# Eight experts of a GNN and FFN kernel: the low halves of the weights all on VectorE, and SiLU in one ScalarE instruction

## What is computed

```python
x1 = x @ W1 + b1                                   # W1: 1024 x 512 for each of 8 experts
x2 = jnp.clip(x @ W2 + b2, -20.0, 20.0)            # W2: 1024 x 512
hidden = jnp.clip(x1 * (x2 * jax.nn.sigmoid(x2)), -10000.0, 10000.0)
return jnp.clip(hidden @ Wo + bo, -10000.0, 10000.0)   # Wo: 512 x 1024
```

## Time and profile before

| what | value |
|---|---|
| median of 3 runs | 579.73 us (577.4 to 579.78) |
| span of the profiled execution | 574.8 us |
| TensorE busy | 514.5 us (89%) |
| VectorE busy | 430.0 us (75%) |
| ScalarE busy | 280.2 us (49%) |
| GpSimd busy | 234.6 us (41%) |

### The profile page before, as it was taken

The page is one execution under the profiler, slowest core; times in us unless marked ns, Lnnn a source line. Parts: engine busy times, 40 slices in busy tenths (PEclk is TensorE's granted clock), DMA queues, the critical chain, the costliest instruction groups (busy, mean ns, idle before and its releaser), DMA issues.

```text
span 574.8 us, 6831 instructions
## 1 busy us (share of the span) xinstructions
PE 514.5 (89%) x2579; PEld 444.6 (77%) x2579; DVE 430.0 (75%) x669; ACT 280.2 (49%) x406; POOL 234.6 (41%) x143
## 2 busy tenths in 40 slices
PE   3899999999999998989988886579999999996994
PEld 3899889999999997878877674456777676674773
DVE  6558977734433345889997776866999999997996
ACT  3425313332332235767775013329669659647630
POOL 5000433333333411122226712323686696690762
PEclk9999999999999999889999979569999999998889
DMA  8289763343344331020016233574888988984632
GB/s 315 94 282 343 234 260 121 121 146 98 125 147 146 128 137 70 1 74 1 1 58 210 114 111 109 196 285 175 328 322 310 388 313 324 391 298 180 220 110 111
DMA packets 20929, 106.32 MB, mean 185 GB/s; under 512 B 4720, under 2 KB 5104, under 8 KB 11168
## 3 DMA queue, kind: packets, MB, share of 16 engines
q1 hardware_dynamic: 15328, 91.53, 42.7%
q0 software_dynamic: 3696, 7.96, 4.2%
q10 hardware_dynamic: 1872, 6.39, 3.6%
HBM read 98.96 MB, written 6.91 MB: 184 GB/s over the span
## 4 chain that ended last, share of the span: by engine, by line
PE 52%; DVE 28%; issue 8%; ACT 5%; POOL 4%; DMA 1%; DVEq 0%; ACTq 0%; POOLq 0%
PE ps L1115 46%; DVE lo L728 11%; DVE sg L1031 4%; PE ps L1178 3%; POOL xres L480 2%; PE ps L1218 1%; ACT hi L561 1%; DVE xres L1047 1%; ACT xg L645 1%; DVE y L1001 1%; DVE hh L1038 1%; DVE x2c L1027 1%; DVE xg_lo L988 1%; DVE ht_lo L993 1%; ACT sg L654 1%
## 5 line engine op out<-in xcount | busy, mean ns | idle before, releaser
L728 DVE TENSOR_TENSOR lo<-raw,hi 128x2048 fp32r<-128x2048 f32 x58 | 153.8, 2668 | 54.8 <-ACT hi L561 54.6
L561 ACT ACTIVATE hi<-raw 128x2048 fp32r<-128x2048 f32 x70 | 131.8, 1913 | 77.0 <-PE ps L1115 65.0
L447 POOL DMA_INDIRECT mask_rows<-colf,bits x48 | 55.9, 1164 | 134.7 <-DMA mask_rows<-colf,bits 82.1
L489 POOL TENSOR_TENSOR lo<-raw,hi 128x2048 fp32r<-128x2048 f32 x12 | 64.9, 5408 | 50.5 <-ACT hi L561 50.4
L1115 PE MATMUL ps<-xt_hi,hi 128*128 128x384 f32 x192 | 65.2, 340 | 2.2 <-DVE xt_lo L744 2.2
L1115 PE MATMUL ps<-xt_lo,hi 128*128 128x384 f32 x192 | 65.1, 339 | 0.0
L1115 PE MATMUL ps<-xt_hi,lo 128*128 128x384 f32 x192 | 64.9, 338 | 0.0
L1115 PE MATMUL ps<-hi,xg_hi 128*128 128x512 f32 x128 | 54.3, 425 | 7.2 <-DVE lo L728 5.7
L1115 PE MATMUL ps<-lo,xg_hi 128*128 128x512 f32 x128 | 52.3, 409 | 0.0
L1115 PE MATMUL ps<-hi,xg_lo 128*128 128x512 f32 x128 | 52.2, 408 | 0.0
L455 POOL TENSOR_SCALAR pr<-pr,small 128x384 f32<-128x384 f32 x16 | 19.9, 1246 | 75.0 <-DVE small L853 75.0
(11 more groups left out here) (209 smaller groups left out, 1131.1 us busy)
## 6 DMA issues: line engine op xcount, KB each, us to landing
raw<-in_wf SPq DMA_DIRECT2D x42, 1024.0 KB, 6.3
raw<-in_wg SPq DMA_DIRECT2D x28, 1024.0 KB, 5.5
xfb<-in_wf SPq DMA_DIRECT2D x6, 1024.0 KB, 5.8
src_i<-in_srcb ACTq DMA_DIRECT2D x4, 768.0 KB, 6.2
dst_i<-in_dstb ACTq DMA_DIRECT2D x4, 768.0 KB, 9.0
y_rows<-y SPq DMA_DIRECT2D x6, 512.0 KB, 2.9
xin<-in_x SPq DMA_DIRECT2D x3, 512.0 KB, 4.4
xres<-in_x SPq DMA_DIRECT2D x3, 512.0 KB, 4.2
```

Of the source, the lines that this page charges most:

```text
L447: pool.indirect_dma_start(out=mbuf[:, :], out_offset=bass.IndirectOffsetOnAxis(ap=bits[:, 1, g:g + 1], axis=0), in_=colf[:, 5, g:g + 1], i ...
L489: pool.tensor_tensor(lo[SLOT[c]][:, :], raws[RAW[c]], f32(hi[SLOT[c]][:, :]), ALU.subtract).then_inc(pool_lo_done, 1)
L561: act.activation(hi[SLOT[c]][:, :], raws[RAW[c]], ACT.Copy).then_inc(hi_done, 1)
L728: dve.tensor_tensor(lo[SLOT[c]][:, :], raws[RAW[c]], f32(hi[SLOT[c]][:, :]), ALU.subtract).then_inc(lo_done, 1)
```

## The change

The set `POOL_LO` goes away: all six chunks of a turn are made on VectorE, and GpSimd keeps its gathers, its selections and the two additions at the end. `Sigmoid` on ScalarE becomes `Silu`, and VectorE's product of `x2c` and the sigmoid goes away. In VectorE's loop n2 stands behind the clip as the code already had it, and n3 is moved from behind `hh` to a place ahead of it, behind `xg_lo`. A branch for experts with over 128 tokens is changed in the same way.

```diff
-LO_ON_POOL = (1, 4)
-POOL_LO = {c for c in range(FIRST, CHUNKS - 3) if (c - FIRST) % 6 in LO_ON_POOL} | {CHUNKS - 2}
         def wait_lo(engine, c):
-            engine.wait_ge(pool_lo_done if c in POOL_LO else lo_done, nth(c))
+            engine.wait_ge(lo_done, c + 1)
...
-            def split_lo(c):
-                pool.wait_ge(hi_done, c + 1)
-                pool.tensor_tensor(lo[SLOT[c]][:, :], raws[RAW[c]], f32(hi[SLOT[c]][:, :]), ALU.subtract).then_inc(pool_lo_done, 1)
...
-                for c in range(f0(e) + 3, min(f0(e) + 9, CHUNKS)):
-                    if c in POOL_LO:
-                        split_lo(c)
...
-            def sigmoid(e):
+            def silu(e):
                 act.wait_ge(x2_clipped, e + 1)
-                act.activation(sg[:, :], x2c[:, :], ACT.Sigmoid).then_inc(sig_done, 1)
+                act.activation(sg[:, :], x2c[:, :], ACT.Silu).then_inc(silu_done, 1)
...
-                nxt = [k if FIRST <= k < CHUNKS and k not in POOL_LO else None for k in range(f0(e) + 3, f0(e) + 9)]
+                nxt = [k if FIRST <= k < CHUNKS else None for k in range(f0(e) + 3, f0(e) + 9)]
...
                 if nxt[2]:
                     split_lo(nxt[2])
-                dve.wait_ge(sig_done, e + 1)
-                link(dve.tensor_tensor(sg[:, :], x2c[:, :], sg[:, :], ALU.mult))
                 if e + 1 < NE:
                     tokens_lo(e + 1, (e + 1) % 2)
+                if nxt[3]:
+                    split_lo(nxt[3])
+                dve.wait_ge(silu_done, e + 1)
                 dve.wait_ge(chunk_used, up_chunks(e) + 4)
                 if e:
                     dve.wait_ge(h_turned, e)
                 link(dve.tensor_tensor(hh[:, :], B[0], sg[:, :], ALU.mult))
                 dve.tensor_scalar(hh[:, :], hh[:, :], 10000.0, -10000.0, ALU.min, ALU.max).then_inc(h_ready, 1)
-                for k in nxt[3:6]:
+                for k in nxt[4:6]:
                     if k:
                         split_lo(k)
```

More of the change, by code:

```diff
@@ L90 @@
 LAST = (NE - 2, NE - 1)
-POOL_LO = {c for c in range(FIRST, CHUNKS - 3) if (c - FIRST) % 6 in LO_ON_POOL} | {CHUNKS - 2}
-def nth(c):
-    return sum(1 for k in range(c + 1) if (k in POOL_LO) == (c in POOL_LO))
 def before(c):
@@ L232, in gnn_ffn @@
         hi_done, lo_done, chunk_used = sem("hi_done"), sem("lo_done"), sem("chunk_used")
-        pool_lo_done = sem("pool_lo_done")
         x_in = [sem(f"x_in{t}") for t in range(NT)]
@@ L256, in gnn_ffn @@
         xg_turned, xg_scaled, xg_hi_done, xg_lo_done = sem("xg_turned"), sem("xg_scaled"), sem("xg_hi_done"), sem("xg_lo_done")
-        x2_clipped, sig_done, h_ready, h_turned, ht_hi_done, ht_lo_done = (
-            sem("x2_clipped"), sem("sig_done"), sem("h_ready"), sem("h_turned"), sem("ht_hi_done"), sem("ht_lo_done"))
+        x2_clipped, silu_done, h_ready, h_turned, ht_hi_done, ht_lo_done = (
+            sem("x2_clipped"), sem("silu_done"), sem("h_ready"), sem("h_turned"), sem("ht_hi_done"), sem("ht_lo_done"))
         y_ready, y_stored = sem("y_ready"), [sem("y_stored0"), sem("y_stored1")]
@@ L267, in gnn_ffn @@
         over_sel, over_turned, over_hi, over_lo = sem("over_sel"), sem("over_turned"), sem("over_hi"), sem("over_lo")
-        over_up, over_clipped, over_sig, over_h = sem("over_up"), sem("over_clipped"), sem("over_sig"), sem("over_h")
+        over_up, over_clipped, over_silu, over_h = sem("over_up"), sem("over_clipped"), sem("over_silu"), sem("over_h")
         over_scaled, over_h_turned, over_h_hi, over_h_lo, over_down, over_added = (
@@ L668, in _ @@
                         split_hi(k)
-                sigmoid(e)
+                silu(e)
                 if e + 1 < NE:
@@ L711, in _ @@
                     act.wait_ge(over_clipped, step)
-                    act.activation(sg[:, :], x2c[:, :], ACT.Sigmoid).then_inc(over_sig, 1)
+                    act.activation(sg[:, :], x2c[:, :], ACT.Silu).then_inc(over_silu, 1)
                     act.wait_ge(over_h_turned, step)
@@ L1091, in _ @@
                     dve.tensor_scalar(x2c[:, :], B[1], 20.0, -20.0, ALU.min, ALU.max).then_inc(over_clipped, 1)
-                    dve.wait_ge(over_sig, step)
-                    dve.tensor_tensor(sg[:, :], x2c[:, :], sg[:, :], ALU.mult).then_inc(over_dve, 1)
-                    dve.wait_ge(over_dve, e * (3 * (NT - 1)) + (3 * t - 2))
+                    dve.wait_ge(over_silu, step)
                     dve.tensor_tensor(hh[:, :], B[0], sg[:, :], ALU.mult).then_inc(over_dve, 1)
-                    dve.wait_ge(over_dve, e * (3 * (NT - 1)) + (3 * t - 1))
+                    dve.wait_ge(over_dve, e * (2 * (NT - 1)) + (2 * t - 1))
                     dve.tensor_scalar(hh[:, :], hh[:, :], 10000.0, -10000.0, ALU.min, ALU.max).then_inc(over_h, 1)
@@ L1103, in _ @@
                                       ALU.min, ALU.max).then_inc(over_dve, 1)
-                    dve.wait_ge(over_dve, e * (3 * (NT - 1)) + 3 * t)
+                    dve.wait_ge(over_dve, e * (2 * (NT - 1)) + 2 * t)
                     dve.scalar_tensor_tensor(out=xres[:, t, :], in0=y[:, 0, :], scalar=fr[:, t, 7:8],
```

## The result

The changed kernel takes 569.44 us in the median (567.67 to 570.18, 4 runs), the one before 578.70 in the same series (577.40 to 579.78, 4 runs). The ratio is 0.984 with a 95% interval of 0.9819 to 0.9861: 9.3 us, 1.6%, faster. The forecast was 572.7 with a range of 566.5 to 576.5, so the sign and the range held and the size was 7.0 for 9.3 us.

What follows compares the result with a forecast made beforehand. The prediction took a ring through VectorE and ScalarE to bound each turn, at 21.1 us for 21.8. ht_lo 9.5 us earlier, less 2.5 given back at the end, made 7.0: 579.73 to 572.7 us, range 566.5 to 576.5.

Steps and rivals of the forecast that it cites:

- The reading of the long rows: In the expert turns, VectorE's long low halves and product wait for GpSimd's instructions: 2.8 and 4.05 us a turn.
- The rival on the other side: Long VectorE rows belong to its own instructions: 22 us slower, 602; chance 0.07 together with late transfers.
- The ring: Each expert turn: a loop through VectorE and ScalarE, with n3's high half before hh, sets 21.1 us for 21.8.
- SiLU and the table load: On ScalarE: SiLU costs 0.63 us like the sigmoid; the added 1.28 us table load hides in a wait, costing nothing.
- The positions: Where turns lie: x2c of turn 7 at 533.3, 8.1 us earlier; ht_lo at 542.2 to 542.3, 9.5 earlier.
- The step that failed: From ht_lo to the last clips: 10.4 less 2.15 plus 4.6 for collisions with GpSimd's additions, 12.9 us.
- over long before: At the end: TensorE's last block starts behind y at about 543.6 and finishes long before VectorE's last clips.
- Rival 1: At the end: no collision or cheap ones, ScalarE's scaling perhaps late; up to 4.6 us better, 568.1; chance 0.15.
- The distance to the median: Whole kernel: the median of the runs lies 4.9 us above the profiled execution's span, and that distance is kept.

Runs made afterwards that it cites:

- e1: Kernel before with only SiLU in place of sigmoid and product, low halves left on GpSimd and n3 behind hh: 574.85 us, ratio 0.9933.
- e4: Changed kernel with the low halves n2, n5 and that of turn 7 back on GpSimd, SiLU and order kept: 582.51 us, ratio 1.0052.
- e5: Changed kernel with the low half n2 alone back on GpSimd: 587.14 us, ratio 1.0158.
- e2: Kernel before with the halves moved to VectorE and n3 ahead of hh, sigmoid and product kept: 568.35 us, ratio 0.9829.
- e6: Changed kernel with the low half n5 alone back on GpSimd: 577.15 us, ratio 0.9973.
- e3: Changed kernel with n3 put back behind hh: 562.96 us, ratio 0.9731; run once more, 564.41 us, ratio 0.9754.
- e7: Changed kernel with ten more unused 128x128 transposes on TensorE ahead of its last block: 568.64 us, ratio 0.9845.

## Why the prediction was right, and where it was not

**The reading of the long rows** was right. The product of 4.74 us and the pair of 7.30 were waits for GpSimd: both are gone with GpSimd's halves, and e1 and e4 show the wait on whichever instruction of VectorE stands in its way, nearly always one with two inputs in SBUF. The rival on the other side, that the long rows belonged to their own instructions, gave 602 and is refuted by the result. The lock that the Trainium skill describes (SBUF — State Buffer, "SBUF: two separate sides"), exclusive and held for the whole instruction, agrees with the meetings shown here: e5's n1 waited 4.4 us, nearly a full GpSimd half.

**The ring** was right to 0.1 us: 21.1 forecast, 21.11 to 21.18 measured, and its parts are confirmed by e2 (0.69 us of VectorE added inside the waiting, no effect), e6 (2.2 us removed and a meeting of 2.8 put in, 21.72) and e3 (n3's high half taken out: 20.15, with TensorE busy throughout). TensorE waits where the prediction said, at the transposes of `hh`, but for 0.9 us and not 0.6: the 20.5 that it was said to need, its busy time in a turn of before, is 20.15 in e3. What I did not say is that the ring is a cost of the change: the order with n3 behind `hh` is open to the same kernel and 5 to 6 us faster.

**SiLU and the table load** were right at 0.63 us and nothing.

**The positions** held. x2c of turn 7 lies at 535.41, less the 1.8 us of the attention layer 533.6, for the forecast 533.3. ht_lo lies at 544.22, less 1.8 542.4, for 542.2 to 542.3. The regular turns give little of the gain, 1.5 us from turn 1 to turn 5. The rest is the step from turn 0 to turn 1 (1.6), that from turn 5 to turn 6 with its pair (5.2), and the stretch from x2c of turn 6 to ht_lo (1.0), where TensorE decides in both kernels.

**The step that failed** is the end: 12.9 us from ht_lo to the last clips, of which 4.6 for two full meetings of the row additions. It measured 10.1 (554.33 less 544.22), with none in it that cost VectorE time. I took the gathered rows to lie there when ScalarE came to them; they landed 3.20 us later than that. By the rows two things made them late: the gathers themselves waited for VectorE's two-input instructions, up to 2.0 us each (2.96 for 0.94), which the forecast had left out, and the rows landed 2.5 us behind the last of them. ScalarE's scaling began at 550.6, and GpSimd's additions at 551.82, within VectorE's last row addition (551.18 to 552.46), for whose end GpSimd seems to have waited: its two took 5.37 for some 4.6. The meeting that VectorE felt then fell behind the clips, at 1.2 us, not 4.6. In its place came something that the prediction had called "over long before": TensorE's last block, 7.4 us with part of it at half clock, for which VectorE waited 1.88 us. The rows of before have the same block ending 10.0 us behind ht_lo (561.8 less 551.80), and 0.4 us ahead of the clips; it lies hidden only as long as VectorE loses time in meetings. e7 takes most of that wait away and shows a meeting of 2.1 us behind it.

From ht_lo to the end of the span it is 23.3 us for 23.0 before, so the end gave back 0.3 us where 2.5 had been put; that is the 7.0 for 9.1. Rival 1, fewer meetings at the end (568.1), had the reason right, ScalarE's late scaling, but it is as far off in size, 11.6 us for 9.3. That the forecast came out nearly as well as it did is in part luck: the meetings it counted on were not there, and a wait of 1.88 us that it had ruled out took some of their place.

**The distance to the median** was misread too. I took 4.9 us as what lies around the span. It is 1.7, and the rest is that the profiled execution was a short one, with a higher clock in the attention layer. It did not enter the forecast of the difference.

## What to carry to other kernels

A simple instruction that takes many times as long as its neighbours of the same size is waiting inside itself: look at what GpSimd does in that moment, and do not count its length as work of its engine, nor as what deleting it would gain. Moving work off GpSimd pays by the meetings it removes, also where the receiving engine looks nearly full. When several things are changed at once, run each alone: here one line, an empty `POOL_LO`, was 15 us faster than before, and the three parts together 9. When work is put into an engine's queue, walk the ring that each instruction closes through the other engines: here the place of one low half, ahead of or behind `hh`, was worth 5 to 6 us, for the 9.3 of the whole change.

## What the runs showed of the hardware that was not expected

- A meeting depends on the phase. The same 128x2048 half on GpSimd cost a turn 0 or 4.4 us (e5: 21.1 and 25.5), by whether it began 0.2 us before or behind the point at which VectorE changed instructions. At the end of the kernel the same meeting moved between three instructions from one execution or version to the next (3.43, 3.80, 3.29).
- GpSimd's share is no measure of this: e5, with half of GpSimd's work on low halves gone, is the slowest version (587.14 us).
- GpSimd's gathers wait for VectorE too. In the changed kernel the same gather takes 0.94 us while VectorE reads PSUM, and 1.6 to 3.0 where it begins within an instruction of VectorE that has two inputs in SBUF; it then ends 0.8 us behind that instruction's end (542.00 + 2.96 for 544.15). This is read from the rows; no run changed it.
- A meeting is not for two-input instructions alone. The clip of `hh`, one input and one output in SBUF, took 4.02 us for 0.43 in turn 7 of the kernel before, beside a GpSimd half that ended at 549.40 (4.59 in e1_silu_alone, 3.39 in e4_halves_back). The product `hh` ahead of it, with one of its two inputs in PSUM, kept 0.69 beside the same half:

```profile
544.94 0.69 DVE L1037 TENSOR_TENSOR hh<-ps,sg 128x512 f32<-128x512 f32 x1
545.66 4.02 DVE L1038 TENSOR_SCALAR hh<-hh 128x512 f32<-128x512 f32 x1
```

- TensorE's granted clock fell to half for some 3 us behind the same one-column products and an idle time of 0.7 to 1.2 us in some of these traces and stayed full in others. So one trace with something added there, as e7_warm, can't show what it does to the clock.
